# Moving widening and conv, and the last dense layer, between the two halves of a step in the last pass of a spectral network

## The reference

```python
for i in range(LAYERS):
    x1 = spectral_conv(h, w1, w2)
    x2 = einsum('bchw,oc->bohw', h, conv_w[i]) + conv_b[i]
    h = layer_norm(x1 + x2, ln_g[i], ln_b[i])      # over 32 channels
    if i < LAYERS - 1:
        h = gelu(h)
h = gelu(h @ fc1_w + fc1_b)                        # 32 -> 128
h = gelu(h @ fc2_w + fc2_b)                        # 128 -> 64
h = (h @ fc3_w + fc3_b)[..., 0]                    # 64 -> 1: a token of 64 values per row
```

## Time and profile before

| | us |
|---|---|
| median of 3 runs | 3648.15 |
| lowest, highest | 3635.49, 3648.17 |
| the profiled execution | 3639.14 |
| its span | 3637.3 |

### The profile page before, as it was taken

The page is one execution under the profiler, slowest core; times in us unless marked ns, Lnnn a source line. Parts: engine busy times, 40 slices in busy tenths (PEclk is TensorE's granted clock), DMA queues, the critical chain, the costliest instruction groups (busy, mean ns, idle before and its releaser), DMA issues. The chain is left out here.

```text
span 3637.3 us, 202203 instructions
## 1 busy us (share of the span) xinstructions
PE 3132.9 (86%) x86496; PEld 2151.1 (59%) x86496; DVE 2467.3 (68%) x3756; ACT 2218.8 (61%) x3645; POOL 2127.3 (58%) x1147
## 2 busy tenths in 40 slices
PE   6777777999968999968999958999999986999998
PEld 3555556777756777756777753333333334666666
DVE  6665547888847888847888844444444436999996
ACT  4455445777745777746777736777777773555554
POOL 2322216888847888838888834444444434555554
PEclk8888887999988999979999978999999997999998
DMA  2232234555544556545555641211121111000000
GB/s 83 94 93 93 88 128 131 169 168 168 172 149 135 169 174 171 171 137 146 168 168 172 174 133 47 60 56 52 54 58 54 54 28 41 13 12 12 12 12 9
DMA packets 206411, 366.15 MB, mean 101 GB/s; under 512 B 107186, under 2 KB 124146, under 8 KB 206018
## 3 DMA queue, kind: packets, MB, share of 16 engines
q1 hardware_dynamic: 194610, 350.25, 32.5%
q10 hardware_dynamic: 7920, 10.03, 0.9%
q0 software_dynamic: 3744, 3.84, 0.7%
HBM read 206.31 MB, written 157.71 MB: 100 GB/s over the span
## 5 line engine op out<-in xcount | busy, mean ns | idle before, releaser
L1296 POOL TENSOR_TENSOR rstd<-var,mhalf 128x16 f32<-128x16 f32 x512 | 1537.4, 3018 | 773.9 <-DVE var L1073 767.2
L571 PE MATMUL ps<-d,hp 128*32 128x48 f32 x32768 | 492.9, 211 | 89.7 <-ACT asb L812 41.7
L571 PEld LDWEIGHTS ps<-d,hp 128*32 128x32 f32 x32768 | 410.2, 112 | 207.6 <-issue 106.3
L1073 DVE TENSOR_REDUCE var<-sq 128x16 f32<-128x528 f32 x384 | 402.8, 1050 | 146.3 <-ACT sq L772 146.2
L812 ACT COPY asb<-ps 128x384 f32<-128x384 f32 x512 | 254.3, 497 | 386.9 <-PE ps L571 264.8
L1087 DVE TENSOR_TENSOR zt<-ps,rstd 128x512 f32<-128x512 f32 x512 | 351.4, 686 | 200.0 <-POOL rstd L1296 195.5
L546 PE MATMUL ps<-ident,hp 128*128 128x128 f32 x2048 | 377.9, 309 | 12.7 <-ACT ho L796 10.0
L496 PEld LDWEIGHTS ps<-cwl,hc 64*64 64x64 f32 x16384 | 273.4, 139 | 146.9 <-issue 136.3
L772 ACT ACTIVATE sq<-ps 128x512 f32<-128x512 f32 x512 | 288.0, 599 | 115.4 <-PE ps L496 81.7
L507 PEld LDWEIGHTS ps<-dyi,gt 64*48 64x48 f32 x16384 | 234.7, 125 | 202.0 <-issue 190.0
L479 PE MATMUL ps<-zb,ex 48*128 48x512 f32 x1024 | 303.5, 668 | 53.8 <-issue 34.8
(11 more groups left out here) (171 smaller groups left out, 4881.3 us busy)
## 6 DMA issues: line engine op xcount, KB each, us to landing
h_scratch<-ho SPq DMA_DIRECT2D x256, 512.0 KB
hc<-h_scratch SPq DMA_DIRECT2D x256, 512.0 KB, 4.4
wsb<-in_w SPq DMA_DIRECT2D x64, 288.0 KB
gin<-g_scratch SPq DMA_DIRECT2D x252, 72.0 KB
gin<-g_scratch SPq DMA_DIRECT2D x504, 36.0 KB
g_scratch<-hp SPq DMA_DIRECT2D x32, 192.0 KB, 3.4
g_scratch<-hp ACTq DMA_DIRECT2D x32, 192.0 KB, 4.1
tokens<-wsb SPq DMA_DIRECT2D x256, 4.0 KB
```

The lines of the kernel that those rows point to most:

```text
L571: last = nc.tensor.matmul(a_ps[row:row + 32, 2 * TRIG * k:2 * TRIG * k + 2 * TRIG], hp[b][:, u, 8 * j + k].rearrange("p v r -> p (v r)"), ...
L1073: nc.vector.tensor_reduce(dst, src, axis=AX.X, op=ALU.add).then_inc(var_ready, 1)
L1296: nc.gpsimd.tensor_tensor(rstd[u][:], var[u][:], mhalf[:], ALU.pow).then_inc(rstd_ready, 1)
```

## The change

On TensorE widening and conv move from the second to the first half of a step, between the first and the second dense layer, and the last dense layer moves from the first to the second half. The squares move with conv on ScalarE. `a2` gets a second pair of buffers, chosen by h, and `gelu2` waits for one `fc3_rows` less. VectorE's list of a step is put in a new order: both normalises first, then reduce 0, z copies 0, reduce 1, coefficients, out_copy, z copies 1. POOL's and SyncE's programs are the same.

```diff
         a2 = [sb(f"a2{k}", [128, 2, 512]) for k in range(2)]
+        a2h = [a2, [sb(f"a2h{k}", [128, 2, 512]) for k in range(2)]]
...
-                        last = nc.tensor.matmul(f3_ps[row:row + 32], fc3[:], a2[k][:, u, :],
+                        last = nc.tensor.matmul(f3_ps[row:row + 32], fc3[:], a2h[h][k][:, u, :],
...
                         if heads:
                             fc1_rows(*heads, k)
-                        if k == 0 and (d := where(i, p, h, 3)):
-                            fc3_rows(*d)
-                        if k == 1 and behind(i, p, h, 0, 2):
+                        if k == 0 and behind(i, p, h, 0, 2):
                             widen(s, p, g, h)
                             conv(s, p, g, h)
+                        if k == 1 and (d := where(i, p, h, 3)):
+                            fc3_rows(*d)
                         if heads:
                             fc2_rows(*heads, k)
...
-                at_least(act, f3_psr, 2 * g + h)
-                nc.scalar.activation(a2[k][:], f2_ps, ACT.Gelu, bias=fc2b[:]).then_inc(a2_ready, 1)
+                at_least(act, f3_psr, 2 * g + h - 1)
+                nc.scalar.activation(a2h[h][k][:], f2_ps, ACT.Gelu, bias=fc2b[:]).then_inc(a2_ready, 1)
...
-                        if k == 1 and behind(i, p, h, 0, 2):
+                        if k == 0 and behind(i, p, h, 0, 2):
                             square(s, 2 * i + p, h, 0)
                             square(s, 2 * i + p, h, 1)
...
                     if c:
                         normalise(s, *c, 0)
-                    if d := where(i, p, h, 3):
-                        out_copy(*d, 1 - p if h else p)
-                    if c:
                         normalise(s, *c, 1)
-                    if nxt:
-                        z_copy_last(1 - p, *nxt, 0)
-                    if h == 1 and (soon := where(i, p, 0, -4)):
-                        coefficients(p, soon[0])
                     if behind(i, p, h, 0, 2):
                         reduce(s, 2 * i + p, h, 0)
                     if nxt:
-                        z_copy_last(1 - p, *nxt, 1)
+                        z_copy_last(1 - p, *nxt, 0)
                     if behind(i, p, h, 0, 2):
                         reduce(s, 2 * i + p, h, 1)
+                    if h == 1 and (soon := where(i, p, 0, -4)):
+                        coefficients(p, soon[0])
+                    if d := where(i, p, h, 3):
+                        out_copy(*d, 1 - p if h else p)
+                    if nxt:
+                        z_copy_last(1 - p, *nxt, 1)
```

## The result

| | before | after |
|---|---|---|
| median of 20 runs each, us | 3649.63 | 3638.18 |
| lowest, highest | 3635.49, 3661.66 | 3629.45, 3649.71 |
| ratio, 95% interval | | 0.9968 (0.9955 to 0.9981) |
| the profiled execution | 3639.14 | 3645.79 (span 3643.9) |

The change takes 0.32% off (11.5 us; the interval is 7 to 16 us). Forecast were 3642 us and a gain of about 5. The profiled execution of after happens to be one of its slower ones: its last pass began 13 us later than that of before, in stages whose code is the same. So the two are compared within the pass. From its first inverse transform (2161.87 and 2175.21) to its last output copy (3001.27 and 3004.73) it takes 839.4 us before and 829.5 after: 9.9 less. In a second profile of the changed kernel (e9) it is 832.1, 7.3 less.

What follows compares the result with a forecast made beforehand. The prediction took a 12.54 us loop through transposes ahead of widening as the bound, the dense chain just under it. Terms - 9.9 - 1.0 + 2.4 + 3.3 = - 5.2 us; forecast 3642 us, range 3626 to 3656.

Steps and rivals of the forecast that it cites:

- The loop and what takes its place: Last pass: widening-to-widening cycle through POOL's powers, normalises and transposes falls from 12.51 to 10.83 us; step becomes 12.32, gaining 9.9.
- dense chain: First layer, gelu, second layer, gelu, next first layer, unable to overlap: halves of 6.50 and 5.82, 12.32 us a step.
- The tail: VectorE's coefficient copy and both normalises ahead of widening: hidden with 0.12 us to spare; cost taken as 0, at most 5 us.
- rival 1: The wait only changes place: VectorE's tail makes widening 0.1 to 0.25 us late a step, 5 to 13 us back; chance 0.15.
- Rival 2: Slower: added delay between copy and normalises; over 0.5% slower if normalises come 0.57 us later than reckoned; chance 0.06.
- the milder rival: VectorE ops wait for an empty pipe, so full spacings: widening 0.05 us late each step, 3 us less gain; chance 0.04.
- The text operations: Three 2.75 us VectorE ops now delay widening 2.63 us each; with the same 6.1 us low-clock cost, 2.4 us lost.
- The fill: Start of the last pass: second dense layer queues behind widening, so step 3 begins 1.6 to 4.7 us later; 3.3 taken.
- The other steps: Nine steps around the 52 of the loop: the same gain of 0.19 us in five of them, 1.0 us.
- Buffers, drain, SyncE: Doubled a2, last two steps, and SyncE's stores and loads with ample cover: costed at nothing.
- Rival 3: More gain by the clock: text and fill stops leave it up, 6.1 and 1.7 us more, 3634 us; chance 0.11.
- Rival 4: Transposes did not hold the step, which stays at 12.5 us; only fill and text terms left, 3654 us; chance 0.04.

Runs made afterwards that it cites:

- e9: The changed kernel as it is, run again on the chip of the text-move kernels: median 3635.37 us, 0.9968 of the kernel before.
- e1: Kernel before, with POOL's powers in the last pass cut to 8 of 16 columns: 12.324 us a step, from 12.513.
- e2: Changed kernel with POOL's powers in the last pass cut to 8 of 16 columns: 12.325 us a step, against 12.330 and 12.325 with full powers.
- e3: Changed kernel with half of the 1 x 1 convolution left out in the last pass: 11.859 us a step, 0.47 less.
- e7: Changed kernel with the last dense layer back in the first half, ahead of widening and conv: 13.285 us a step, 0.96 more.
- e8: Changed kernel with a third 2.90 us POOL power in each step of the last pass: 13.713 us a step.
- e4: Changed kernel with one more VectorE op between the second coefficient copies and the normalises: 12.549 us a step, 0.22 later.

## Why the prediction was right, point by point

- *The loop and what takes its place.* Right in mechanism and size: 12.51 to 12.33 was measured, 12.32 forecast; - 9.5 us, forecast - 9.9. The hundredths are partly luck: the dense chain came out 0.03 shorter than forecast, 12.29, and the loop's turn put 0.04 on it. e1 and e2 show that the loop was the cause, e3 and e7 that the dense chain is what is left, e8 that the new loop has the length of its links.
- *The tail.* The forecast took 0 of a possible 5 us and counted 0.12 us of cover. In the ordinary steps the two spacings are 0.41 and 0.59, as reckoned to 0.02, and e4 leaves 0.06 to 0.08 us of cover. Taking 0 was too good for the first step of a turn: there the normalises start 0.24 us later than in the others and W is 0.17 late. That is rival 1 in one step of four, at the place that it named; it takes back 2 us where the rival had 5 to 13. Rival 2 needed the normalises 0.57 us later, and nothing of that size is there. For the milder rival the forecast read "VectorE: DVE Perf Modes" ("The DRAIN you can't avoid") in the Trainium skill as full spacings, 0.49 behind the start of the copies and 0.69 between the normalises. The trace has 0.41, and 1.28 for both ops, which is 0.59 apart. The section also says that a next op that is not held starts earlier, and with that the trace agrees.
- *The text operations.* This term was mis-sized: + 2.4 forecast, - 1.2 measured. The stop was right (2.64 us longer than a step without it, 2.63 forecast). Of the 3.6 us off, most is the clock: the forecast carried over the 6.1 us that the low clock had cost before, and it cost 3.1 (1.52 and 1.58). The rest are the plain steps: in this written-out part they take 12.13 us (with the stop, 14.77) and not the 12.32 of the loop.
- *The fill.* + 3.3 forecast within + 1.6 to + 4.7; + 2.3 in one profile, + 3.6 in the other. The 1.3 between the two lie behind the third widening, where the granted clock is 0.86 in the one and 0.77 in the other. The cause, the second dense layer now queued behind a widening that must wait, shows as the wait of 2.19 us at 2206.60.
- *The other steps.* - 1.0 forecast; - 1.5 measured in one profile and + 0.1 in the other. In the other the last 24 us of the pass ran at a granted clock of 0.93, and from step 60 to the end it took 72.9 us instead of 71.4.
- *Buffers, drain, SyncE.* Costed at nothing, and no wait for a load appears in the steady waits. The drain has no measurement of its own; it is within the - 1.5 and + 0.1 of the line above.
- *The sum.* - 5.2 against - 9.9 and - 7.3 in the pass's two profiles. The median lay at 3638, 4 us below the forecast 3642, inside the range. But the forecast gain of 5 is outside the 7 to 16 us measured. The text term explains 3.6 of it, and the 11.5 of the medians are again above the 9.9 and 7.3 that the two profiles of the pass show. Rival 3 (the clock stays up) came half true: the low clock of the text steps cost 3.1 us instead of 6.1. Rival 4 is out by e1.

## What to carry to other kernels

Where an item goes round through several engines, write down the cycle link by link, and ask which instructions are in it only because they stand ahead in a queue: swapping them out is worth just the distance to the next chain, here 0.18 of 12.5 us, however much the cycle itself shrinks (12.5 to 10.8). Count beside the steady state what is rare. Three 2.75 us operations in 64 steps cost about as much as the 52 steady steps gave back, since each stood in front of a wait that TensorE hangs on and the low clock came on top; an idle place of the same engine a few steps earlier took them for nothing. And where a chain is hidden with a tenth of a microsecond to spare, look at the step in which the hardware loop turns: it is the one that shows first. Last, a part that is harmful alone (widening moved without the last layer, + 0.8 us a step) can be needed for the whole.

## What the runs showed of the hardware

- POOL's power takes 1.64 us on 8 columns, 2.90 on 16 and 6.60 on 39; from these, an estimate of about 0.16 us a column and 0.4 fixed.
- Chips differed by 4.6% on the same program (3645 and 3485 us). Where the kernel before took 3485 us, the first 500 us ran at a granted clock of 0.96 with 137 GB/s moved (profile of e1), where it took 3645 at 0.84 with 90 GB/s (e9). In the last pass the loop of the change takes 12.325 us on both (e2, whose shorter powers are off the path, and e9), so the difference lies in other stages; why, no run here shows.
- The clock fell to 1.2 GHz for a short while behind some stops of TensorE of 2.6 us and not behind others of the same length: in the first profile of the change in the intervals behind the first and second stop, in the second profile (e9) in those behind the second and third.
- In a hardware loop, the first VectorE op of a new turn started 0.65 us behind the start of the two copies ahead of it, where the same op in the middle of a turn started 0.41 behind them. It was so in 12 of 12 turns back, with the full powers and with the short ones of e2.
